# A two-layer graph network with a mixture of experts: seven and thirteen late node tiles in place of five and eleven

## The reference

```
def rgcn_gate_layer(x, row, col, edge_type, basis, att, gate_w, root, bias):
    w = jnp.einsum('rb,bio->rio', att, basis)            # 30 bases -> 2 relation weights of 512x512
    x_j = x[col]
    for r in range(2):
        gate = jax.nn.sigmoid(x_j @ gate_w[r, :, 0])
        msgs.append(gate[:, None] * x_j @ w[r])
    msg = jnp.where((edge_type == 0)[:, None], msgs[0], msgs[1])
    agg = jax.ops.segment_sum(msg, row, num_segments=x.shape[0])
    return agg + x @ root + bias

n = _layernorm(x)
h = jax.nn.relu(rgcn_gate_layer(n, ...layer 1))
x = x + rgcn_gate_layer(h, ...layer 2)
t = _layernorm(x)
# two shared and eight routed experts of width 64 (top 2 of a softmax), gelu between
x = x + shared(t) + routed(t)
```

## Time and profile before

| | |
|---|---|
| median of 3 runs | 1653.71 us (1652.87 to 1659.6) |
| profiled execution, its own time | 1661.87 us |
| its span | 1660.2 us, 23968 instructions |
| PE busy | 1575.4 us (95%), 7903 matmuls |
| DVE, ACT, POOL busy | 892.5 us (54%), 720.0 us (43%), 441.5 us (27%) |
| mean granted TensorE clock | 0.99 |
| moved by DMA | 274.24 MB, mean 165 GB/s |

### The profile page before, as it was taken

The page is one execution under the profiler, slowest core; times in us unless marked ns, Lnnn a source line. Parts: engine busy times, 40 slices in busy tenths (PEclk is TensorE's granted clock), DMA queues, the critical chain, the costliest instruction groups (busy, mean ns, idle before and its releaser), DMA issues. The chain is left out here.

```text
span 1660.2 us, 23968 instructions
## 1 busy us (share of the span) xinstructions
PE 1575.4 (95%) x7903; PEld 1232.0 (74%) x7903; DVE 892.5 (54%) x2178; ACT 720.0 (43%) x1169; POOL 441.5 (27%) x570
## 2 busy tenths in 40 slices
PE   4999999989898999999999888999999999999998
PEld 3667666777786667677887666787888787878787
DVE  3555587867742333346655356555555554555543
ACT  2344445656642222234656425445344534453442
POOL 3573232467742000000667332011001100110000
PEclk9999999999999999999999999999999999999999
DMA  8899999487758999996777671342234323422201
GB/s 261 251 279 281 293 295 293 147 214 124 127 78 226 301 282 277 281 288 215 160 128 136 130 209 26 119 107 79 77 120 103 82 76 118 107 79 76 89 26 45
DMA packets 74565, 274.24 MB, mean 165 GB/s; under 512 B 12966, under 2 KB 12980, under 8 KB 59362
## 3 DMA queue, kind: packets, MB, share of 16 engines
q1 hardware_dynamic: 50514, 206.19, 39.9%
q0 software_dynamic: 23952, 66.83, 22.1%
HBM read 179.82 MB, written 92.76 MB: 164 GB/s over the span
## 5 line engine op out<-in xcount | busy, mean ns | idle before, releaser
L937 ACT ACTIVATE th<-bank 128x512 fp32r<-128x512 f32 x158 | 94.4, 597 | 191.4 <-PE bank L1171 187.8
L1151 PE MATMUL bank<-tth,w1h 128*128 128x512 f32 (+1 forms) x400 | 164.5, 411 | 0.0
L1151 PE MATMUL bank<-w2h,gth 128*128 128x512 f32 x395 | 157.9, 400 | 0.0
L1151 PE MATMUL bank<-ttl,w1h 128*128 128x512 f32 (+1 forms) x400 | 156.3, 391 | 0.0
L1151 PE MATMUL bank<-tth,w1l 128*128 128x512 f32 (+1 forms) x400 | 155.3, 388 | 0.0
L1151 PE MATMUL bank<-w2l,gth 128*128 128x512 f32 x395 | 154.3, 391 | 0.0
L1151 PE MATMUL bank<-w2h,gtl 128*128 128x512 f32 x395 | 154.0, 390 | 0.0
L1151 PE MATMUL bank<-root2h,th 128*128 128x512 f32 x316 | 132.2, 418 | 8.3 <-DVE yout L1476 5.0
L1151 PE MATMUL bank<-root1h,th 128*128 128x512 f32 x316 | 132.6, 420 | 7.0 <-DVE yout L1476 5.2
L1447 DVE SCALAR_TENSOR_TENSOR tl<-bank,th 128x512 fp32r<-128x512 f32 x79 | 54.5, 689 | 144.9 <-ACT th L937 141.6
L1151 PE MATMUL bank<-root1l,th 128*128 128x512 f32 x316 | 125.8, 398 | 0.0
(11 more groups left out here) (213 smaller groups left out, 3745.2 us busy)
## 6 DMA issues: line engine op xcount, KB each, us to landing
basis_t<-in_gnn_basis SPq DMA_DIRECT2D x64, 896.0 KB
xin<-in_x SPq DMA_DIRECT2D x39, 512.0 KB
xin<-y SPq DMA_DIRECT2D x39, 512.0 KB
out<-zr SPq DMA_DIRECT2D x19, 1024.0 KB, 3.9
y<-yout SPq DMA_DIRECT2D x37, 512.0 KB
z<-yout SPq DMA_DIRECT2D x34, 512.0 KB
zr<-in_x SPq DMA_DIRECT2D x16, 1024.0 KB, 4.9
zr<-z POOLq DMA_DIRECT2D x16, 1024.0 KB, 8.0
```

What stands on the lines that cost most here:

```text
L937: act.activation(th_a[:, s, :], tpb[s][:], f).then_inc(s_hi, 1)
L1151: ins = pe.matmul(out_ap, a(k), b(k), start=first, stop=last)
```

## The change

LATE goes from 5 to 7 and LATE2 from 11 to 13, so node loops end after 72 and 66 tiles and two more tiles of each layer come behind its edge pairs. Late pairs get a buffer each: in the first layer two in `yout` and the third in `gx`; in the second two in `yout`, then `late_eh` and `late_el` (the places of `eh` and `el`), `xn_a` and `late_out`. Each late pair of the second layer has a semaphore of its own, and ACT waits for pairs 2 and 3 before it writes `tn`, which lies where they do. The second layer's split begins at step 62; the first layer's stays at 68. Two more blocks of 128 rows of `y` and of `z` are zeroed. The statistics of three late tiles, not one, are taken in the last step of SA. Pair 37 of the second layer is loaded behind the edges. What DVE does for the expert stage keeps its distance from the end of the late tiles, and POOL's add of `x` comes behind four late pairs, not three.

```diff
-    TURN_AT, REPEATS_AT, W_SPLIT_AT = 34, 42, [68, 64]
+    TURN_AT, REPEATS_AT, W_SPLIT_AT = 34, 42, [68, 62]
...
-    LATE, LATE2 = 5, 11
+    LATE, LATE2 = 7, 13
...
+        late_eh, le = place("late_eh", [P, 2, H], at=eh_at)
+        late_el, _ = place("late_el", [P, 2, H], at=le)
...
-        def late2_buffer(g):
-
-            k = (g - NC // 2) % 4
-            return (yout[:, k % 2, :, :], k) if k < 2 else ((xn_a, late_out)[k - 2][:, :, :], k)
+        def late_buffer(layer, g):
+
+            k = g - (NC // 2 if layer else NA // 2)
+            if k < 2:
+                return yout[:, g % 2, :, :]
+            if layer == 0:
+                return gx[:, 2 * k - 4:2 * k - 2, :]
+            return (late_eh, late_el, xn_a, late_out)[k - 2][:, :, :]
...
-            for g in range(NG - 1, NG + 1):
+            for g in range(NC // 2 + 4, NG + 1):
                 sp.wait_ge(s_tp, Step(SE, Pos(2 * (g - 4) + 1)).T.k + 1)
                 load_pair(SE, Pos(g))
...
-            for g in LATE2_PAIRS[:3]:
+            for g in LATE2_PAIRS[:4]:
                 add_late2(g)
             pool.wait_ge(s_zx, 1)
             add_x(Pos(1))
-            for g in LATE2_PAIRS[3:]:
+            for g in LATE2_PAIRS[4:]:
                 add_late2(g)
-                if g == LATE2_PAIRS[3]:
+                if g == LATE2_PAIRS[4]:
                     group_rstd(Pos(0))
...
+            for s in s_late2[2:4]:
+                act.wait_ge(s, 16)
             q_norm(Pos(0))
...
-                if st.phase == SE and st.g.k - 4 in LATE2_PAIRS and not apart:
-                    dve.wait_ge(s_late2[0], 16)
-                elif st.t.mod(2) == 0 and not apart and (st.phase != SE or late2_buffer(st.g.k)[1] < 2):
+                late = st.t.k - (NC if st.layer else NA) if st.phase in (SL, SE) else 0
+                if st.t.mod(2) == 0 and late < 4:
                     wait(dve, s_ystore[st.gg.mod(2)], buffer_free(st.gg.mod(2), st.gg))
...
                     if st.t.k + 1 == NA:
-                        pair_stats(late_steps[-1])
+                        for late in late_steps[4:]:
+                            pair_stats(late)
...
-                elif i == FC + 2:
+                elif i == LATE2 - 4:
                     add_first()
-                elif i == FC + 3:
+                elif i == LATE2 - 3:
                     q_stats(Pos(0), range(QT), True)
```

More of the change, by code:

```diff
@@ L91, in gnn_moe_kernel @@
     QLAST = 3
-    LATE, LATE2 = 5, 11
+    LATE, LATE2 = 7, 13
     NA, NC = NT - LATE, NT - LATE2
-    assert NA % 2 == 0 and LATE < 8 and NC % QT == 0
+    assert NA % 2 == 0 and NC % 2 == 0
     A0, B0, L0, C0 = 0, NA, NA + ET, NT + ET
@@ L304, in gnn_moe_kernel @@
         s_late = sem("late_rows_added")
-        s_late2 = [sem(f"late_rows_added{i}") for i in range(5)]
+        s_late2 = [sem(f"late_rows_added{i}") for i in range((LATE2 + 1) // 2)]
         s_gx = [sem(f"gathered{i}") for i in range(6)]
@@ L474, in gnn_moe_kernel @@
         LATE2_PAIRS = range(NC // 2, NG)
-        def late2_buffer(g):
-            k = (g - NC // 2) % 4
-            return (yout[:, k % 2, :, :], k) if k < 2 else ((xn_a, late_out)[k - 2][:, :, :], k)
+        def late_buffer(layer, g):
[5 more added lines that the diff above has]
+            return (late_eh, late_el, xn_a, late_out)[k - 2][:, :, :]
         def late2_added(eng):
-            for k in range(5):
-                eng.wait_ge(s_late2[k], 16 * (len(LATE2_PAIRS[k::4]) if k < 4 else 1))
+            for s in s_late2:
+                eng.wait_ge(s, 16)
         def is_tail(st):
@@ L858, in _ @@
                 pool.wait_ge(s_y, 2 * g + 2)
-                pool.dma_start(pair_rows(y1, Pos(g), 2), yout[:, g % 2, :, :], accum_op=ALU.add).then_inc(s_late, 16)
+                pool.dma_start(pair_rows(y1, Pos(g), 2), late_buffer(0, g), accum_op=ALU.add).then_inc(s_late, 16)
             pool.wait_ge(s_y, NT)
@@ L871, in add_late2 @@
             def add_late2(g):
-                rows, k = late2_buffer(g)
                 pool.wait_ge(s_y, NT + 2 * g + 2)
-                pool.dma_start(pair_rows(z, Pos(g), 2), rows, accum_op=ALU.add).then_inc(s_late2[k], 16)
+                pool.dma_start(pair_rows(z, Pos(g), 2), late_buffer(1, g),
+                               accum_op=ALU.add).then_inc(s_late2[g - NC // 2], 16)
             def group(q):
@@ L902, in _ @@
             add_x(Pos(1))
-            for g in LATE2_PAIRS[3:]:
+            for g in LATE2_PAIRS[4:]:
                 add_late2(g)
-                if g == LATE2_PAIRS[3]:
+                if g == LATE2_PAIRS[4]:
                     group_rstd(Pos(0))
             pool.wait_ge(s_y, 2 * NT)
-            pool.dma_start(z[TAIL + again:N, :], scratch[again:P, :], accum_op=ALU.add).then_inc(s_late2[4], 16)
+            pool.dma_start(z[TAIL + again:N, :], scratch[again:P, :], accum_op=ALU.add).then_inc(s_late2[-1], 16)
             group_rstd(Pos(1))
@@ L1471, in y_out @@
                     target = scratch[:] if st.layer else xn_e[:, 0, :]
-                elif st.phase == SE:
-                    target = late2_buffer(st.g.k)[0][:, st.t.mod(2), :]
+                elif st.phase in (SL, SE):
+                    target = late_buffer(st.layer, st.g.k)[:, st.t.mod(2), :]
                 else:
```

## The result

| kernel | median | runs | ratio to the kernel before |
|---|---|---|---|
| before | 1656.86 us | 11 (1652.87 to 1662.41) | |
| changed | 1663.46 us | 11 (1658.35 to 1666.85) | 1.0036, 95% interval [1.002, 1.0053] |

The change costs 6.0 us by the ratio (3.3 to 8.8). The forecast was 2.3 us more and no change that can be told; 0.36% is within the 0.5% named there, and the interval reaches just past it. In absolute us the median lies 0.5 above the upper end of the range; the kernel before, run beside it, took 3.2 us more than in the three runs shown at first, and a range moved up by that holds the result. So the direction was right and the size too small by 3.7 us.

The account below looks back on a forecast made before the run. TensorE was taken as the bound, busy 1575.4 of 1660.2 us, so only waits could change. Terms 4.0 + 1.0 - 3.5 - 1.0 + 1.8 = 2.3 us, added to the 1653.71 us median, gave 1656.0 us; range 1647 to 1663.

Parts of the forecast that it names:

- first layer: stall, shift, and the rows to clear: First layer, nodes to edges: 4.0 us lost as PE's stall grows from 0.98 to 5.3; clearing more rows loses 1.0.
- late tiles to product 2: Late tiles to second layer: first load of y in time, a new wait of 2.3 us for the second; 3.5 us gained.
- first pairs of the second layer: Second layer's first pairs: PE's 1.30 us wait for a y_out at 553 shrinks in a lighter crowd; 1.0 us gained.
- second layer's weights: Second layer, nodes to edges: the earlier split waits for its weights' load, delaying a y_out PE wants; 1.8 us lost.
- costed at nothing: Late tiles to experts, group loads, ACT's new wait before tn, own buffers and pair 37's load: 0 us.
- rival (b): Late tiles to second layer: second load slow as before, clock falls, only 0.8 us gained; 1659.2 us; chance 0.15, shared.
- rival (d): First layer, behind the new 5.3 us stall: slow clock with nothing hidden, 2.5 us more; 1658.5 us; chance 0.07.
- rival (c): Second layer's split: the weights' load takes 11.1 us, so that term is 8.1 us; 1662.3 us; chance 0.11.

Follow-up runs that it names:

- before_zero: The kernel before, with two more blocks of 128 rows cleared in each layer's list, into a spare table: ratio 1.0 to the kernel before.
- late13: The changed kernel with only the second layer's part: 13 late tiles there, 5 in the first layer: ratio 1.0003 to the kernel before.
- late7: The changed kernel with only the first layer's part: 7 late tiles there, 11 in the second layer, split from step 64: ratio 1.0044 to the kernel before.
- sp_first: The changed kernel, with SP issuing the second layer's first two loads of y one behind the other: ratio 1.0031 to the kernel before.
- few_added: sp_first, with the late rows' adds to y cut to 8 of 128 partitions: ratio 1.002 to the kernel before.
- gathers_later: sp_first, with six gathers of the second layer's first edge rows put off to products 16, 24 and 32: ratio 0.9989 to the kernel before.
- before_split70: The kernel before, with the first layer's relation weights split two steps later, in steps 70 to 73: ratio 1.0004 to the kernel before.

## Why the prediction was wrong in size

Measured terms are means over the profiles of this case where the code of the stage is the same: before, before again, `before_zero` and `late13` against the changed kernel, `late7`, `sp_first`, `few_added` and `gathers_later` in the first layer; for products 0 to 9 the six kernels with 5 late tiles in the first layer against the five with 7 and SP's old order.

| step of the prediction | forecast | measured |
|---|---|---|
| first layer: stall, shift, and the rows to clear | +5.0 | +3.4 (p46-T1 +1.1, T1-T2 +4.5, T2-L -2.2) |
| late tiles to product 2 | -3.5 | +0.1 (L-p0 -2.3, p0-p2 +2.4) |
| first pairs of the second layer | -1.0 | -1.7 |
| second layer's weights | +1.8 | +1.4 |
| costed at nothing | 0 | +1.6, unsure by 1 |
| sum | +2.3 | +4.8; timed +6.0 (3.3 to 8.8) |

The sum is nearer than its terms, by luck: 3.6 us were missed at the late tiles and 1.6 behind product 60, and 2.7 came back from the other three, which each cost less or won more than forecast. For the same reason rival (b), whose 5.5 us lie next to the timed 6.0, isn't borne out term by term: its 5.0 for the first layer measured 3.4.

- **First layer.** The stall was foretold as 5.3 us and is 5.49, in each kernel of that code within 0.05. What failed is the sentence that the shift goes whole through the edges: 2.2 of the 4.5 us came back there. Some 1.3 of them are the waits for el that before has at 351.88 and 363.31 (1.67 and 3.81 us) and that were 2.06 and 2.13; the rest isn't traced. On the other side 1.1 us were lost ahead of the first turn, where I had said that nothing differs: the first edge pairs' steps count from the end of the loop and so come two tiles sooner, and one product-to-product interval there is 5.9 to 6.1 us where it was 5.12: the row at its end shows PE waiting for DVE's yout, 0.52 us at 265.31 in before and 1.54 at 254.27 now. No run tests what makes that wait longer. Nor is the 1.1 firm: `late13`, with the first layer's tiles of before, has 103.90 in this column too. The slow stretch of rival (d) came (0.72 in 312 to 318) and was hidden, as the forecast held: the second turn took 3.32 us (313.72 to 317.04) for 1.98 (318.67 to 320.65), and the 1.46 us that PE waited for DVE behind it are gone. Clearing rows, put at 1.0, shows no cost in `before_zero`, whose timing can't tell 1.0 from 0.
- **Late tiles to second layer: the step that failed.** I took 7 us for the second load because the first load and two adds had left the crowd, and a new wait of 2.3. It took 10.6 us, PE waited 5.66 and came out at the lower clock: the price of rival (b), whose condition, the DMA share of 1.01 in the earlier trace rows, I had read and weighed too lightly. The load gained nothing from the traffic that left: the DMA share was 1.01 to 1.07 in every 5 us from 505 to 520 all the same. `sp_first` and `gathers_later` are what shows it: an earlier issue of that load won nothing by product 9 (42.7 us against 42.3), and six gathers fewer ahead of product 9 won 6.4 (36.3). So what bounds the stretch is what is to be moved ahead of product 9, not the time at which that load is issued. It isn't bytes alone: gathers and adds are about 1.5 MB each, and taking away the adds won 3.4. By the Trainium skill (TensorE: Matmul & The Clock Gate, "HAM oscillation") a long enough wait for data lets the clock fall, and the next burst begins slow. The prediction used this at the first stall; here too the trace agrees: the burst after the wait of 5.66 us began at 0.50.
- **First pairs and weights.** Both as foretold within 0.7 us: PE's wait for yout at 553.26 is gone, and the weights' load, the mechanism of rival (c), took its short time of 4.5 us. The price of that rival was misread: the four loads behind the median of 11.1 us are of two sizes. The first of each layer carries 1792 KB and took 17.3 and 17.5 us, the second 256 KB and took 4.3 and 4.8, so two of four took longer, not three, and none took 11.1. In all 14 profiles the second layer's second load took 4.3 to 5.1 us: (c) had almost no chance of its 8.1 us. From product 62 to the second edge turn of that layer it is 22.3 to 22.9 us in all eight kernels with 13 late tiles (the moved tiles added) and 21.1 to 21.2 in the others.
- **Costed at nothing.** ACT's wait for pairs 2 and 3 was hidden in the changed kernel; `late7` shows its price when it isn't (5.0 us). The 1.6 us are what is left behind product 60 (913.0 us to the end, mean of the eight kernels with 13 late tiles, against 910.0 of five with 11, `late7` left out; less the 1.4). They vary by as much from one execution to the next. Some 1.1 of them go along with the clock: between p60 and e it lacks 8.0 us of full speed in the mean of the eight and 6.8 in that of the five. No run tests that.
- **Between profiles and timed runs** 1.2 us stay open. The mean granted clock of the timed runs is 0.9861 in the changed kernel and 0.9879 in 27 runs of before (those beside `late7`; 0.9875 to 0.9889 in the four sets beside experiments); 0.0018 of 1660 us is 3.0 us. That goes along with the loss but doesn't explain it: `before_split70` had 0.9869 against 0.9889 and lost 0.7 us.

## What to carry to other kernels

Where the DMA share of a stretch is 1.0, don't price a load that is issued sooner, or a wait that is removed, until you have said which bytes leave the stretch: here a new order won 7 us and gave them back within seven tiles, and putting off 1.5 MB that nobody wanted for 190 us kept them. A wait of the bounding engine for another that has been behind for several steps may be a debt: here moving some of the lagging engine's work elsewhere changed the wait by 2.3 to 3.1 us and the time by nothing clear of the error. A median of landing times is worth nothing before the sizes behind it are looked at. And before two profiles 6 us apart are compared stage by stage, take the kernel before a second time; the stages that repeat to hundredths are the ones to argue from.

## What the chip did that I had not expected

- A slow stretch of PE costs about the same each time. The product behind the wait at 519.92 took from 520.65 to 525.5, 4.9 us for 2.8; read in stretches of 2 us over the whole span, the granted clock of each profile lacks 9 to 14 times about 1.7 us of full speed, and number and places differ between executions of the same kernel (before, up to 530 us: at 42, 364 and twice at 514; again: at 356, 506 and twice at 514). The same wait ends both ways: in before the granted clock was 0.50 in 44 to 46, behind a wait of 1.71 us at 43.36; in before, again, it stayed 1.00 in 42 to 46, behind one of 1.72 at 41.26. Over the four sets of 17 to 29 runs of before the mean clock and the time go together (correlations of -0.43 to -0.71), so I take this for a part of the 10 us and more between runs; no run tests it.
- The same load of 512 KB takes 4.0 us at the head of the crowd and, one place behind, 10.4 (before), 12.3 (before, again: issued at 503.90, PE has it at 516.16) and 10.6 us (changed), whether or not the first load and the adds of the late rows stand beside it.
- From 560 to 620 us the second layer's node loop has a DMA share of 0.92 to 1.02, and PE loses nothing by it: six more gathers there cost 0.05 us. SP issues the loop's loads four pairs ahead; I take that for the reason that it rides full queues and its start, where nothing is ahead, doesn't, but no run changes the distance.
